# Ternary weight quantization of an SSM and feed-forward kernel: every second slice on GpSimd instead of VectorE

## The reference, cut to what matters

```python
def _weight_quant(w):
    scale = jnp.clip(jnp.mean(jnp.abs(w)), EPS_W)
    return jnp.clip(jnp.round(w / scale), -1, 1) * scale

def _bitlinear(x, w, b):
    xn = _layer_norm(x)
    xq = _activation_quant(xn)
    wq = _weight_quant(w)
    return jnp.einsum('bsd,fd->bsf', xq, wq) + b
```

## Time and profile before

| what | value |
| --- | --- |
| median of 2 runs | 11817.86 us (11803.73 to 11832.0) |
| profiled execution, own time | 11845.11 us |
| its span (slowest core, core 5) | 11843.2 us |
| spans of the 8 cores | 11788.8 to 11843.2 us |
| granted TensorE clock, mean by core | 0.664 to 0.673 |
| w1 stage, in the span | 655.3 to 1299.5 us |
| w2 stage, in the span | 1299.5 to 1899.1 us |

### The profile page before, as it was taken

The page is one execution under the profiler, slowest core; times in us unless marked ns, Lnnn a source line. Parts: engine busy times, 40 slices in busy tenths (PEclk is TensorE's granted clock), DMA queues, the critical chain, the costliest instruction groups (busy, mean ns, idle before and its releaser), DMA issues.

```text
span 11843.2 us, 84780 instructions; the slowest of 8 cores (11788.8 to 11843.2 us)
## 1 busy us (share of the span) xinstructions
PE 5205.5 (44%) x21976; PEld 3064.2 (26%) x21976; DVE 5405.4 (46%) x7116; ACT 2530.6 (21%) x6860; POOL 1903.4 (16%) x2469
## 2 busy tenths in 40 slices
PE   2023336134152623525152351138888722278880
PEld 1011114133141512414141241013333211133330
DVE  1034442755737376473737647763333355510003
ACT  1543442212222121221212122111111122200000
POOL 0000000422414142241414224000000000000000
PEclk5555557666676666667676666568888855589995
DMA  6854443010020201102020110111111122255455
GB/s 217 295 189 159 175 168 126 0 47 36 0 82 0 82 0 43 39 0 82 0 82 0 43 40 0 46 47 73 66 66 66 57 106 104 102 161 160 158 163 172
DMA packets 131091, 1022.88 MB, mean 86 GB/s; under 512 B 16386, under 2 KB 16642, under 8 KB 45442
## 3 DMA queue, kind: packets, MB, share of 16 engines
q1 hardware_dynamic: 91060, 781.51, 19.6%
q0 software_dynamic: 39568, 235.96, 5.0%
HBM read 781.47 MB, written 235.93 MB: 86 GB/s over the span
## 4 chain that ended last, share of the span: by engine, by line
PE 30%; DVE 28%; DMA 16%; issue 12%; ACT 11%; SPq 1%; DVEq 0%; ACTq 0%; POOL 0%; POOLq 0%
PE pb L484 9%; PE pb L949 8%; DVE hcb L572 7%; PE pb L592 6%; DVE hbf L560 6%; ACT aub L542 5%; DMA g_s<-gb 5%; DMA wsl<-w 3%; DMA gr<-g_s 2%; PE pb L521 2%; ACT gb L788 1%; DVE gbn L794 1%; PE pbf L343 1%; ACT stg L396 1%; DVE xq2b L898 1%
## 5 line engine op out<-in xcount | busy, mean ns | idle before, releaser
L592 PE MATMUL pb<-identT,hcb 128*128 128x128 f32 x4096 | 743.4, 358 | 3172.2 <-DVE dxx L580 3122.3
L560 DVE TENSOR_TENSOR_SCAN hbf<-aub,hst 128x256 f32<-128x256 f32 x2048 | 1637.8, 839 | 1087.2 <-ACT aub L542 991.3
L592 PEld LDWEIGHTS pb<-identT,hcb 128*128 128x128 f32 x4096 | 692.6, 193 | 3202.8 <-issue 3202.8
L550 POOL TENSOR_TENSOR aub<-dxt,bbf 128x256 f32<-128x256 f32 x1024 | 787.7, 774 | 3199.9 <-DVE hbf L560 1730.4
L776 PE MATMUL pb<-wq1s,xq1t 128*128 128x512 bf16 x4096 | 1065.8, 420 | 173.8 <-ACT gb L788 173.6
L542 ACT ACTIVATE aub<-dtb,anegT 128x256 f32<-128x256 f32 x2048 | 982.5, 506 | 699.4 <-DVE hbf L560 602.9
L484 PE MATMUL pb<-xlt,wxt 128*128 128x256 f32 (+1 forms) x4352 | 1032.0, 404 | 6.1 <-DVE xlt L468 5.4
L949 PE MATMUL pb<-wq2s,xq2r 128*128 128x512 bf16 x4096 | 905.0, 382 | 180.0 <-DMA xq2r<-xq2t_s 180.0
L572 POOL TENSOR_TENSOR hcb<-hbf,cbf 128x256 f32<-128x256 f32 x1024 | 895.0, 906 | 448.4 <-DVE hst L566 448.4
L484 PEld LDWEIGHTS pb<-xlt,wxt 128*128 128x128 f32 (+1 forms) x4352 | 865.5, 199 | 171.7 <-issue 12.7
L572 DVE TENSOR_TENSOR hcb<-hbf,cbf 128x256 f32<-128x256 f32 x1024 | 827.4, 875 | 23.2 <-DVE hst L566 22.4
(11 more groups left out here) (142 smaller groups left out, 5609.2 us busy)
## 6 DMA issues: line engine op xcount, KB each, us to landing
wxt<-wxpt_s SPq DMA_DIRECT2D x136, 1024.0 KB, 4.8
wsl<-w SPq DMA_DIRECT2D x128, 1024.0 KB, 5.3
wsl<-w SPq DMA_DIRECT2D x64, 2048.0 KB, 8.8
xq2r<-xq2t_s SPq DMA_DIRECT2D x64, 2048.0 KB, 10.3
g_s<-gb POOLq DMA_DIRECT2D x256, 256.0 KB, 2.3
gr<-g_s SPq DMA_DIRECT2D x64, 1024.0 KB, 4.9
wq1t_s<-stg POOLq DMA_DIRECT2D x16, 2048.0 KB, 7.8
wq2t_s<-stg POOLq DMA_DIRECT2D x16, 2048.0 KB, 7.2
```

The source lines that it names most:

```text
L550: ut = S.comp(eng_u, lambda e, dh=dh, n=n, slot=slot: e.tensor_mul(aub[:, (4 + slot) * TC:(5 + slot) * TC], dxt[:, dh * TC:(dh + 1) * TC], ...
L560: e.tensor_tensor_scan(out=hbf[:, hb0 + n * TC:hb0 + (n + 1) * TC], data0=aub[:, slot * TC:(slot + 1) * TC], data1=aub[:, (4 + slot) * TC: ...
L592: e.matmul(bank[:, tt * 128:(tt + 1) * 128], hcb[:, n * TC + tt * 128: n * TC + (tt + 1) * 128], ident[:, :], start=(n == 0), stop=False, ...
```

## The change

The odd slices of both stages are quantized by POOL, the even ones still by VectorE. POOL gets three buffers of its own (`wqbP`, `wc1P`, `wabsP`), so there are now two quantized slices at a time. The waits that were on the slice before are now on the slice two before, which is the last one of the same engine: the first comparison waits for the subtraction of slice - 2, the subtraction for the last transpose of slice - 2. The transposes read the buffer of the engine that made the slice. Loads, transposes, copies, stores and their order are as they were.

```diff
+    wqbP = sb(W1, "wqbP", 128, 4096, BF16)
+    wc1P = sb(W1, "wc1P", 128, 4096)
+    wabsP = sb(W1, "wabsP", 128, 4096)
...
-            c1 = S.comp("dve", lambda e, sl=sl: e.tensor_scalar(
-                out=wc1[:, 0:D], in0=ws[:, sl * 4096:sl * 4096 + D],
+            qe = "dve" if si % 2 == 0 else "pool"
+            qc1, qab, qqb = ((wc1, wabs, wqb) if qe == "dve" else
+                             (wc1P, wabsP, wqbP))
+            c1 = S.comp(qe, lambda e, sl=sl, qc1=qc1: e.tensor_scalar(
+                out=qc1[:, 0:D], in0=ws[:, sl * 4096:sl * 4096 + D],
                 scalar1=ws1v[:, 0:1], scalar2=0.5, op0=ALU.mult, op1=ALU.is_ge),
-                waits=[lt, tw1] + opt(f"w1qm_{si-1}"), tag=f"w1q1_{si}")
+                waits=[lt, tw1] + opt(f"w1qm_{si-2}"), tag=f"w1q1_{si}")
...
-            qm = S.comp("dve", lambda e: e.tensor_sub(
-                wqb[:, 0:D], wc1[:, 0:D], wabs[:, 0:D]),
-                waits=[c2] + opt(f"w1tp_{si-1}_{ND-1}"), tag=f"w1qm_{si}")
+            qm = S.comp(qe, lambda e, qc1=qc1, qab=qab, qqb=qqb: e.tensor_sub(
+                qqb[:, 0:D], qc1[:, 0:D], qab[:, 0:D]),
+                waits=[c2] + opt(f"w1tp_{si-2}_{ND-1}"), tag=f"w1qm_{si}")
...
-                    bank[:, 0:128], wqb[:, dc * 128:(dc + 1) * 128],
+                    bank[:, 0:128], qqb[:, dc * 128:(dc + 1) * 128],
...
-            qm = S.comp("dve", lambda e: e.tensor_sub(
-                wqb[:, :], wc1[:, :], wabs[:, :]),
-                waits=[c2] + opt(f"w2tp_{s2-1}_31" if s2 >= 1 else
-                                 f"w1tp_63_{ND-1}"), tag=f"w2qm_{s2}")
+            qm = S.comp(qe, lambda e, qc1=qc1, qab=qab, qqb=qqb: e.tensor_sub(
+                qqb[:, :], qc1[:, :], qab[:, :]),
+                waits=[c2] + opt(f"w2tp_{s2-2}_31" if s2 >= 2 else
+                                 f"w1tp_{62 + s2}_{ND-1}"), tag=f"w2qm_{s2}")
```

More of the change, by code:

```diff
@@ L328, in build_nc @@
                 tag=f"w1l{si}")
-            c1 = S.comp("dve", lambda e, sl=sl: e.tensor_scalar(
-                out=wc1[:, 0:D], in0=ws[:, sl * 4096:sl * 4096 + D],
+            qe = "dve" if si % 2 == 0 else "pool"
[3 more added lines that the diff above has]
+                out=qc1[:, 0:D], in0=ws[:, sl * 4096:sl * 4096 + D],
                 scalar1=ws1v[:, 0:1], scalar2=0.5, op0=ALU.mult, op1=ALU.is_ge),
-                waits=[lt, tw1] + opt(f"w1qm_{si-1}"), tag=f"w1q1_{si}")
-            c2 = S.comp("dve", lambda e, sl=sl: e.tensor_scalar(
-                out=wabs[:, 0:D], in0=ws[:, sl * 4096:sl * 4096 + D],
+                waits=[lt, tw1] + opt(f"w1qm_{si-2}"), tag=f"w1q1_{si}")
+            c2 = S.comp(qe, lambda e, sl=sl, qab=qab: e.tensor_scalar(
+                out=qab[:, 0:D], in0=ws[:, sl * 4096:sl * 4096 + D],
                 scalar1=ws1v[:, 1:2], scalar2=0.5, op0=ALU.mult, op1=ALU.is_gt),
-                waits=[c1] + opt(*(["m2_a31"] if si == 0 else ())),
+                waits=[c1] + opt(*(["m2_a31"] if si <= 1 else ())),
                 tag=f"w1q2_{si}")
-            qm = S.comp("dve", lambda e: e.tensor_sub(
-                wqb[:, 0:D], wc1[:, 0:D], wabs[:, 0:D]),
-                waits=[c2] + opt(f"w1tp_{si-1}_{ND-1}"), tag=f"w1qm_{si}")
+            qm = S.comp(qe, lambda e, qc1=qc1, qab=qab, qqb=qqb: e.tensor_sub(
+                qqb[:, 0:D], qc1[:, 0:D], qab[:, 0:D]),
+                waits=[c2] + opt(f"w1tp_{si-2}_{ND-1}"), tag=f"w1qm_{si}")
             for dc in range(ND):
                 bank = pbf[dc % 2]
-                tp = S.comp("pe", lambda e, dc=dc, bank=bank: e.matmul(
-                    bank[:, 0:128], wqb[:, dc * 128:(dc + 1) * 128],
+                tp = S.comp("pe", lambda e, dc=dc, bank=bank, qqb=qqb: e.matmul(
+                    bank[:, 0:128], qqb[:, dc * 128:(dc + 1) * 128],
                     identb[:, :], start=True, stop=True, is_transpose=True),
@@ L372, in build_nc @@
                 tag=f"w2l{s2}")
-            c1 = S.comp("dve", lambda e, sl=sl: e.tensor_scalar(
-                out=wc1[:, :], in0=ws[:, sl * 4096:(sl + 1) * 4096],
+            qe = "dve" if s2 % 2 == 0 else "pool"
+            qc1, qab, qqb = ((wc1, wabs, wqb) if qe == "dve" else
+                             (wc1P, wabsP, wqbP))
+            c1 = S.comp(qe, lambda e, sl=sl, qc1=qc1: e.tensor_scalar(
+                out=qc1[:, :], in0=ws[:, sl * 4096:(sl + 1) * 4096],
                 scalar1=ws2v[:, 0:1], scalar2=0.5, op0=ALU.mult, op1=ALU.is_ge),
-                waits=[lt, tw2] + opt(f"w2qm_{s2-1}" if s2 >= 1 else "w1qm_63"),
+                waits=[lt, tw2] + opt(f"w2qm_{s2-2}" if s2 >= 2 else
+                                      f"w1qm_{62 + s2}"),
                 tag=f"w2q1_{s2}")
-            c2 = S.comp("dve", lambda e, sl=sl: e.tensor_scalar(
-                out=wabs[:, :], in0=ws[:, sl * 4096:(sl + 1) * 4096],
+            c2 = S.comp(qe, lambda e, sl=sl, qab=qab: e.tensor_scalar(
+                out=qab[:, :], in0=ws[:, sl * 4096:(sl + 1) * 4096],
                 scalar1=ws2v[:, 1:2], scalar2=0.5, op0=ALU.mult, op1=ALU.is_gt),
                 waits=[c1], tag=f"w2q2_{s2}")
-            qm = S.comp("dve", lambda e: e.tensor_sub(
-                wqb[:, :], wc1[:, :], wabs[:, :]),
-                waits=[c2] + opt(f"w2tp_{s2-1}_31" if s2 >= 1 else
-                                 f"w1tp_63_{ND-1}"), tag=f"w2qm_{s2}")
+            qm = S.comp(qe, lambda e, qc1=qc1, qab=qab, qqb=qqb: e.tensor_sub(
+                qqb[:, :], qc1[:, :], qab[:, :]),
+                waits=[c2] + opt(f"w2tp_{s2-2}_31" if s2 >= 2 else
+                                 f"w1tp_{62 + s2}_{ND-1}"), tag=f"w2qm_{s2}")
             for fl in range(32):
@@ L388, in build_nc @@
                 bank = pbf[fl % 2]
-                tp = S.comp("pe", lambda e, fl=fl, bank=bank: e.matmul(
-                    bank[:, 0:128], wqb[:, fl * 128:(fl + 1) * 128],
+                tp = S.comp("pe", lambda e, fl=fl, bank=bank, qqb=qqb: e.matmul(
+                    bank[:, 0:128], qqb[:, fl * 128:(fl + 1) * 128],
                     identb[:, :], start=True, stop=True, is_transpose=True),
```

## The result

The changed kernel takes 12227.18 us in the median of 11 runs (12173.54 to 12277.17), the kernel before 11817.8 in 10 runs beside it (11777.11 to 11876.48). The ratio is 1.0341, with a 95% interval from 1.031 to 1.0372: 409 us slower. The forecast was 11655 and the range ended at 12120.

A forecast was written before the change was run, and what follows sets the result against it. Subtraction and transposes, alternating on one quantized buffer, were taken to bound both stages. Savings of 110 us in w1 and 54 in w2, 164 together, gave 11681 for the profiled execution and 11655 for the median; range 11625 to 12120.

The forecast's parts named there:

- What bounds the kernel: In w1 and w2, waits between VectorE's subtraction and the transposes bound the stages, 644.2 and 599.6 us long.
- The ring of subtraction and transposes: In w1 and w2, one quantized buffer makes subtraction and transposes wait for each other: 172.8 and 153.1 us of waits.
- forecast ceiling of 181 us: Most that two quantized buffers could save: 110 us in w1 and 71 us in w2.
- The ring through POOL: POOL's stores and quantizing share one program: store, quantize, transposes, next store; forecast w2 period 33.7 us instead of 37.12.
- The formulas for the two periods: Shortest store-to-store times in w1 and w2, summing POOL's comparisons, subtractions and waits, plus 7.2 or 13.4 us to the store.
- s: POOL's time for one comparison of 128x2048, assumed 2.5 us, with 2.3 and 9.8 us as ends.
- I take half a subtraction's price, 2.5 us: POOL's comparison of 128x2048 assumed at 2.5 us (4.9 at 4096), since one operand is read instead of two.
- slow comparisons: Rival: two-pass comparisons on POOL at 9.8 us, periods 57.4 us in w1 and 62.3 in w2, +675 us, 12490; chance 0.23.
- The two engines take turns: Rival: VectorE and POOL block each other, periods 37.9 us in w1 and 42.8 in w2, +51 us, 11870; chance 0.12.
- VectorE's cluster: VectorE's subtraction and next two comparisons, starting some 20 us after the store, when POOL is done in w2 or waiting in w1.
- A store that lands after 7 to 8 us: In w1 and w2, landing later than 7 to 8 us after issue was named as a sign the forecast was wrong.
- The clock: Rival: TensorE's clock, 0.50 in both stages, rises to 2.4 GHz, saving another 236 us, 11400; chance 0.03.

The follow-up runs named there:

- e5: As e2, but loads that e2 issues around a store wait until that store has landed; 11626.9 us, ratio 0.9829 to the kernel before.
- e7: Changed kernel, but POOL quantizes its odd slices by rounding with a large constant, min and max, without comparisons; 11639.1 us, ratio 0.9857 to the kernel before.
- e1: Changed kernel with its two sets of buffers, but VectorE quantizes every slice and POOL only issues stores; 11647.0 us, ratio 0.9853 to the kernel before.
- e4: Changed kernel, but the second operation of all four comparison instructions is an addition of 0.5; 11656.9 us in one run.
- e9: As e7, but POOL's last instruction of a slice, a single addition, also multiplies by 1.0; 11746.8 us in one run.
- e8: Changed kernel with VectorE's three instructions of each even slice cut to 64 columns, POOL's unchanged; 12223.4 us in one run.
- e2: Changed kernel, but VectorE makes all comparisons and POOL only the subtractions of odd slices; 11801.5 us, ratio 0.9989 to the kernel before.
- e6: As e1, with stores alternating between two staging buffers in both stages; 11394.8 us, ratio 0.9641 to the kernel before.
- e11: As e6, with four transposed blocks copied by one ScalarE instruction; 11330.8 us, ratio 0.9588 to the kernel before.

## Why the prediction was wrong

**What bounds the kernel: right.** The ring of subtraction and transposes was there, and opening it was worth what was reckoned, once the store is left alone. Against a forecast ceiling of 181 us the stages gained 196 in e5 and 179 in e7, with periods of 32.9 and 32.2 us (e5) where 33.5 and 32.7 were worked out (the store lands after 7.0 and 6.6 us there, where 7.84 and 7.1 were taken). e1, where the loads slow the store, gained 126 in the stages.

**The ring through POOL: right.** The formulas for the two periods, which leave s open, give 46.8 and 52.5 us at the measured s = 7.16. Measured are 48.5 and 52.6. The agreement in w2 is closer than the formula deserves: the two comparisons are 0.5 us less than 4s (14.06 each) and the subtraction is 0.5 us over the 9.6 assumed. In w1 the period shown above is 48.0, with 0.45 us for a late load and 1.5 for the two stretched instructions, neither of which the formula has, less 0.8 because an undisturbed subtraction is 4.49 and not 4.9.

**The step that failed is "I take half a subtraction's price, 2.5 us".** Measured are 7.16 us for 128x2048 and 14.06 for 128x4096, nearly three times that, and above the 6.3 from which the kernel is 2% slower by the prediction's own working. The value lies between the bounds named there (2.3 and 9.8), in the "slow comparisons" rival, which had a chance of 0.23 and whose price of 9.8 was too high (by the prediction's own formula its w2 period would be 63.1, not 62.3, and its time about 12505). The reason given, one operand instead of two, leads near the mark for two arithmetic operations: 1.98 us in e4 and 1.90 in e9. It does not for a comparison, nor for an instruction with one operation. No row of the kernel before shows POOL comparing, and the argument leant on an instruction that does something else. The range, which should have reached to the price of 9.8 or at least to its middle, stopped at s = 6.7 (6.8 by its own sum).

The rule of the Trainium skill quoted there ("GPSIMD Engine Reference", section 4.1: one-input work at about line rate) pushed the same way. e4, e7 and e9 agree with it for two arithmetic operations (1.9 to 2.0 us for 2048 elements); the changed kernel's 7.16 us and e7's 5.36 do not. The two-input price of section 3.1 there, 4497 ns for 2048 elements, is what L344 takes at best, 4492.

**"The two engines take turns": right as a mechanism, small as a cost.** It was priced at 9.7 and 9.1 us a period, if all of VectorE's work fell into POOL's ring. 1.9 and 1.3 us are on the path (e8). The reason given for a low price was that POOL would be done or waiting when VectorE's cluster starts. That did not come true, since POOL's comparisons are so long: VectorE's comparisons in w1 take up to 8.0 us in every second of its slices. The cost is small for another reason: nobody waits for VectorE. In the w1 rows each of VectorE's three instructions ends 1.1 to 2.2 us after POOL's, about what it needs alone. This agrees with the Trainium skill ("SBUF — State Buffer", "Who interferes with whom"): one waits for the other's whole instruction.

**A store that lands after 7 to 8 us: right for the changed kernel (6.6), wrong as a rule.** It hung on the loads' timing, which the prediction looked at for POOL's load in w2 only. In e1 and e2, where VectorE is early, the loads slide onto the store (medians of 10.3 and 8.3, and of 12.0 and 13.1 us).

**The clock: right.** It is 0.50 in both stages before and after, and in e6 and e11 too. The "17 of 33.5 us" that the prediction gives for TensorE should be 14.3 (228.81 us of w1 over 16 groups), which changes nothing.

## What to carry to other kernels

Before an instruction is moved to another engine, its price there has to be measured for the very operations that it has, in one small run: here the pair multiply and compare cost 7.16 us and multiply and add 1.98 on the same tile and engine, and that decided between 1.4% faster (e7) and 3.4% slower. Separate what a change bundles: here the second buffer brought the gain, and the comparisons on the engine that came with it the loss. When a producer gets early, look at what it releases: loads that start sooner can slow the one store that is on the path (from 7 us to 12 or 13). And compare the changed stages by themselves: e1's time met its forecast with a quarter of the gain coming from stages that nobody had touched.

## What the runs showed of the hardware that was not expected

- On POOL an instruction of 128x2048 float32 with a scalar takes 1.9 to 2.0 us for two arithmetic operations (multiply and add in e4, min and max in e7, add and multiply in e9), 5.4 us for one operation of either kind (addition 5.36, comparison 5.44), and 7.16 us for two with a comparison in either place. A superfluous second operation made the single addition 2.8 times faster. At 4096 columns: 3.68, 10.6 and 14.06 us.
- VectorE's subtraction of 64 columns, 226 ns alone, lasted up to 11.2 us beside POOL (e8).
- A 2 MB store issued by POOL lands after 6.6 us in the median with no load in flight beside it (e5, w2), and after 12 and 13 us in the median where one load was issued 2 or 4 us before it and another 0.5 us after it (e2). With the loads 4 us before and 4 us after it, 7.8 us (the kernel before, w1).
